# Cross attention in a two-layer decoder: scores from plain queries and keys of two heads at a time, in the two halves of the rows

## The reference, cut to what matters

```python
        q = lat @ Wq
        kv_input = jnp.concatenate([x, lat], axis=1)
        kv = kv_input @ Wkv
        k, v = jnp.split(kv, 2, axis=-1)
...
        dots = jnp.einsum('bhid,bhjd->bhij', q, k) * scale
        attn = jax.nn.softmax(dots, axis=-1)
        out = jnp.einsum('bhij,bhjd->bhid', attn, v)
```

## Time and profile before

| | us |
|---|---|
| median of 3 runs | 941.05 (939.36 to 941.20) |
| the profiled execution | 941.59, of it a span of 939.7 |
| busy in the span: PE / DVE / ACT / POOL | 847.7 / 561.1 / 480.4 / 256.1 |
| busy weight loads (PEld) | 695.7 |
| cross attention, from its first score to the first of its last unit | 132.2 to 519.1 |

### The profile page before, as it was taken

The page is one execution under the profiler, slowest core; times in us unless marked ns, Lnnn a source line. Parts: engine busy times, 40 slices in busy tenths (PEclk is TensorE's granted clock), DMA queues, the critical chain, the costliest instruction groups (busy, mean ns, idle before and its releaser), DMA issues.

```text
span 939.7 us, 19518 instructions
## 1 busy us (share of the span) xinstructions
PE 847.7 (90%) x6498; PEld 695.7 (74%) x6498; DVE 561.1 (60%) x1561; ACT 480.4 (51%) x1154; POOL 256.1 (27%) x541
## 2 busy tenths in 40 slices
PE   5999879999999999999999968885897888887788
PEld 3888668888888888888888756663796566665565
DVE  3876466555655566655655347774544577666474
ACT  2455465555555555555555315664464476677141
POOL 3864120000000000000000047551075577776110
PEclk9999999999999999999999989999899899999995
DMA  7000000000000000000000030001222000000000
GB/s 270 2 2 1 1 1 1 1 1 1 0 0 0 0 0 0 0 0 0 0 0 0 1 115 1 2 1 28 88 47 59 1 1 0 0 0 0 24 1 22
DMA packets 9410, 15.85 MB, mean 17 GB/s; under 512 B 816, under 2 KB 5040, under 8 KB 8976
## 3 DMA queue, kind: packets, MB, share of 16 engines
q1 hardware_dynamic: 8400, 13.23, 4.2%
q0 software_dynamic: 960, 1.97, 0.9%
HBM read 13.16 MB, written 2.03 MB: 16 GB/s over the span
## 4 chain that ended last, share of the span: by engine, by line
PE 76%; ACT 7%; DVE 6%; issue 6%; POOL 3%; DMA 1%; ACTq 1%; DVEq 0%; POOLq 0%; SPq 0%
PE psum L875 9%; PE psum L887 9%; PE psum L855 5%; PE psum L856 5%; PE psum L857 5%; PE psum L847 5%; PE psum L598 4%; ACT arena L1301 4%; PE psum L840 3%; PE psum L617 3%; PE psum L635 3%; PE psum L956 2%; PE psum L566 1%; PE psum L1034 1%; PE psum L648 1%
## 5 line engine op out<-in xcount | busy, mean ns | idle before, releaser
L1818 DVE TENSOR_REDUCE xnegmax<-psum 128x1 f32<-128x768 f32 x128 | 122.4, 956 | 139.5 <-PE psum L857 139.3
L1405 ACT ACTIVATE arena<-psum,xnegmax 128x768 f32<-128x768 f32 x128 | 115.5, 903 | 139.5 <-DVE xnegmax L1818 97.8
L2265 POOL COPY acur<-A_all 128x128 f32 (+1 forms) x18 | 5.2, 293 | 388.1 <-PE psum L840 388.1
L875 PE MATMUL psum<-pack_a,arena 128*128 128x128 f32 x768 | 106.8, 275 | 0.2 <-ACT arena L1396 0.2
L1249 ACT ACTIVATE arena<-psum 128x384 f32<-128x384 f32 (+1 forms) x128 | 69.5, 546 | 71.2 <-PE psum L620 42.1
L855 PE MATMUL psum<-kv_high,xq_high 128*128 128x384 f32 x256 | 101.5, 396 | 1.8 <-DVE kv_low L1813 1.6
L875 PEld LDWEIGHTS psum<-pack_a,arena 128*128 128x128 f32 x768 | 87.5, 141 | 13.9 <-issue 12.3
L1396 ACT ACTIVATE arena<-psum 128x512 f32<-128x512 f32 x128 | 75.9, 593 | 42.5 <-PE psum L875 42.5
L887 PE MATMUL psum<-arena,xv 128*64 128x256 f32 x768 | 89.9, 383 | 0.0
L856 PE MATMUL psum<-kv_low,xq_high 128*128 128x384 f32 x256 | 86.8, 339 | 0.0
L857 PE MATMUL psum<-kv_high,xq_low 128*128 128x384 f32 x256 | 86.7, 339 | 0.0
(11 more groups left out here) (309 smaller groups left out, 1853.6 us busy)
## 6 DMA issues: line engine op xcount, KB each, us to landing
w1all<-in_w SPq DMA_DIRECT2D x1, 2048.0 KB, 8.2
arena<-in_w SPq DMA_DIRECT2D x1, 2048.0 KB, 10.8
pack_v<-in_pack_v SPq DMA_DIRECT2D x1, 1088.0 KB, 9.0
pack_l<-in_pack_l SPq DMA_DIRECT2D x1, 1079.5 KB, 12.0
pack_q<-in_pack_q SPq DMA_DIRECT2D x1, 1024.0 KB, 6.9
pack_a<-in_pack_a SPq DMA_DIRECT2D x1, 653.0 KB, 6.1
pack_f<-in_pack_f SPq DMA_DIRECT2D x1, 556.0 KB, 9.9
x<-in_x SPq DMA_DIRECT2D x2, 256.0 KB, 3.0
```

The lines of the kernel that those rows point to most:

```text
L875: last = transpose(bank[4 + (3 * u + c) % 2][:, (2 * i + h) * P:(2 * i + h + 1) * P], xprob[:, u % 2, h * KEYS + kt * P:h * KEYS + (kt + 1 ...
L1405: activation(xprob[:, u % 2, half * KEYS:(half + 1) * KEYS].rearrange("p (c w) -> p c w", c=2), src, ACT.Exp, bias=xnegmax[:, u % 2, half: ...
L1818: v.tensor_reduce(xnegmax[:, u % 2, half:half + 1], banks_pair(half), AX.XY, ALU.max, negate=True)\
```

## The change

The head products `A_all` go away. For each pair of heads TensorE now forms plain queries (128 columns: two heads of 64) and plain keys of the 768 rows, the keys by three split matmuls for each half of 384 (`keys`), one such half in every unit, ahead of their use, in bank 7. Queries and keys are split again (`xq_high`, `k_high` by ScalarE, `xq_low`, `k_low` by VectorE), now inside the loop. A unit is now two heads with one tile of 128 queries: each head's product runs over 64 rows only, one in the lower and one in the upper half of the rows, into different PSUM banks, and all twelve score matmuls of a unit stand together. The key weights are split once ahead of the loop (`wk_all`), and GpSimd copies the two heads' columns for each pass.

```diff
-                def queries(it, u):
-                    pe.wait_ge(sx["acur_ready"], it * 2 + u % 2 + 1)
-                    mm(bank[6][:, T:2 * T], acur[:, u % 2, :], kvT[:, u // 2, S2:KEYS], start=True, stop=True)\
-                        .then_inc(sx["q_psum"], 1)
+                def queries(it, b):
+                    pe.wait_ge(sx["wq_ready"], it + 1)
+                    mm(bank[6][:, T:2 * T], wq_now[:, :], kvT[:, b, S2:KEYS], start=True, stop=True).then_inc(sx["q_psum"], 1)
+                def keys(it, b, c):
+                    pe.wait_ge(sx["wk_ready"], it + 1)
+                    out, some = bank[7][:, 0:W], slice(c * W, (c + 1) * W)
+                    mm(out, wk_now[:, 0, :], kv_high[:, b, some], start=True, stop=False)
+                    mm(out, wk_now[:, 0, :], kv_low[:, b, some], start=False, stop=False)
+                    mm(out, wk_now[:, 1, :], kv_high[:, b, some], start=False, stop=True).then_inc(sx["k_psum"], 1)
...
-                def scores(u, half):
+                def scores(u):
+                    tile, slot = slice(u % 2 * P, (u % 2 + 1) * P), u // 2 % 2
                     for c in range(2):
...
+                        some = slice(c * W, (c + 1) * W)
+                        for i, (q, k) in enumerate(((xq_high, k_high), (xq_high, k_low), (xq_low, k_high))):
+                            for a in range(2):
+                                head = slice(XD * a, XD * (a + 1))
+                                last = mm(bank[2 * a + c][:, 0:W], q[head, slot, tile], k[head, slot, some],
+                                          start=(i == 0), stop=(i == 2))
+                                if c == 1 and i == 2:
+                                    last.then_inc(sx["score_psum"], 1)
```

More of the change, by code:

```diff
@@ L116, in decoder @@
         x = sb("x", [P, NT, D])
+        with nc.sbuf_tensor("k_high", [P, 2, KEYS], f32r) as k_high, nc.sbuf_tensor("k_low", [P, 2, KEYS], f32r) as k_low:
+            pass
         z = sb("z", [P, NT, D])
@@ L927, in body @@
                                 if prev or u >= 4:
[L929 to L935, removed]
-                            if cur:
-                                pe.wait_ge(sx["q_ready"], n + 2)
-                            weighted(it * 4 + b - 1, (b - 1) % 4)
-                        if behind:
+                                    pe.wait_ge(sx["rb_ready"], p - 1)
+                                    pe.wait_ge(sx["y_done"], p)
+                                queries(*after)
+                            pe.wait_ge(sx["k_ready"], n + (4 if prev or u else 3))
+                            values(*after, odd)
+                            if not prev and u == 0:
+                                pe.wait_ge(sx["v_ready"], 3)
+                                keys(0, 1, 1)
+                        if behind and not odd:
+                            transposed(n - 1, (u - 1) % 8, (2,))
+                        if weigh and not odd:
+                            if cur:
+                                pe.wait_ge(sx["q_ready"], p + 2)
+                            weighted(p - 1, (b - 1) % 4, range(0, 2))
+                        if weigh and odd:
+                            weighted(p - 1, (b - 1) % 4, range(2, KT))
+                        if behind and odd:
                             transposed(n - 1, (u - 1) % 8, (2,))
-                        if weigh:
-                            factors(it * 4 + b - 1)
+                        if weigh and odd:
+                            factors(p - 1)
                         if not cur and u == 0:
@@ L1843, in body @@
                             dve.wait_ge(sx["pT_psum"], m * 3 + 2)
-                            v.tensor_copy(xpT[:, (mu // 2) % 2, mu % 2, 2 * T:4 * T], bank[4 + (3 * mu + 1) % 2][:, :])\
+                            v.tensor_copy(xpT_of(mu, 1), bank[4 + (3 * mu + 1) % 2].rearrange("p (k a q) -> p k a q", k=2, a=2))\
                                 .then_inc(sx["pT_dve"], 1)
+                        if cur:
+                            if not odd:
+                                query_low(it * 4 + b + 1, (b + 1) % 2)
+                            values(n + 3, (b + 1) % 4, odd)
+                            if not prev and u == 0:
+                                keys_low(4, 1, 1)
                         if not odd and ((prev and u == 0) or (cur and u)):
```

185 lines of the change are left out of this document (98 added, 87 removed).

## The result

The changed kernel takes 971.78 us (median of 4 runs, 969.67 to 972.88) against 941.12 (939.36 to 941.41): a ratio of 1.031, with a 95% interval of 1.0272 to 1.0348. It is slower, and by twice what was predicted: +30.7 by the medians instead of +15. The profiled execution took 970.9, with a span of 968.6, 28.9 more than before.

The account below looks back on a forecast made before the run. TensorE's work was taken as the bound, 12.315 us a pair. Profiled 941.6, plus 7.9 for two waits in 31 loop pairs, plus 6.9 for the start, gave 956 us; range 935 to 975.

Parts of the forecast that it names:

- the case that was held likeliest: Whole kernel: halves overlap and two waits per pair make it slower, 956 us, range 945 to 966, chance 0.53.
- TensorE's scores: Each unit, first score to first key: two row halves run at once, 1.26 us, bounds 1.06 and 2.31.
- The two waits: TensorE idles before values (0.13 even, 0.49 odd unit) for low keys, and 0.70 before the even weighted sum for low query.
- The rival of a shorter chain: Loop: scores to low query take less time than the rows say; pair 11.84, total 934 us, chance 0.20.
- The loop's sum: Loop: a pair takes 12.57 us, 0.255 more than before; over 31 pairs +7.9 us.
- The price of a switch: TensorE's row or column halves: 0.07 to 0.13 or 0.20 us each; seven a pair, 0.83 us in the sum.
- The start: Ahead of the loop and first unit: second unit starts at 144.2 instead of 137.32, +6.9 us, bounds +4.5 and +9.
- The rival of the clock: Loop: waits lower TensorE's granted clock for a tenth of it; 972 us, chance 0.12 together with further waits.
- No overlap: Score matmuls: the two halves don't run at once in fp32r, 2.31 us per unit; 1021 us, chance 0.07.
- nothing to see: Loop: chain shorter by just 0.24 us a unit, pair 12.1; total within 0.2% of before, chance 0.08.

Follow-up runs that it names:

- both heads in one half: The changed kernel with both heads' score matmuls in the lower half of the rows, the second head's scores left out: 1042.31 us in one run.
- the idle matmuls: The changed kernel plus nine matmuls with unread results in TensorE's waits ahead of the loop and in its first unit: 966.72 us.
- both moves: The changed kernel with the low query right behind the second maximum, high query before the first exponential, and odd units' weighted passes ahead of the values: 937.59 us.

## Why the prediction was right on the sign and wrong on the size

The measured 971.78 lies inside the range that was given, 935 to 975, but above the 945 to 966 of the case that was held likeliest. The mechanism came as forecast; two terms of the sum were too small.

- **TensorE's scores.** From first score to first key 1.24 (predicted 1.26). The halves overlap; shown with both heads in one half. That the sum of 1.26 came out is in part luck: it had six steps of 0.176 and a switch, and left out that the first step is 0.28, as the first of a group over all rows was 0.27 before.
- **The two waits.** They came at the places named, with the releasers named. The values of the odd unit start 1.95 behind the first key (predicted 1.98), the low query 3.29 (3.32). The rival of a shorter chain is out: the chain is as long as the rows made it.
- **The loop's sum was mis-sized: +7.9 predicted, +19.3 measured**, a pair of 12.94 instead of 12.57 (401.08 / 31). The pair above has 12.95, and its terms differ from the predicted ones by 0.38. *Low query to weighted sum:* 494.31 + 0.41 to 494.97 is 0.25, and I had taken a hand-over of 0.05; with the 0.04 that the low query is early, 0.16. TensorE's list has three waits in a row there, of which the low query is the first: the trace has two instructions of its queue, lines 890 and 892, at 494.8 and 494.9, and the weight load behind them at 494.94. Ahead of the values in the odd unit no such instruction stands between the low keys and the weight load, at 499.18. *Transposes and factors to the scores:* 0.80 (501.93 to 502.73) instead of 0.63, because from the factors to the first score it takes 0.31 (489.47 to 489.78) instead of 0.14 to matmuls over all rows before (501.76, below, to 501.90 in the earlier trace rows): 0.17. *Values and weighted sum of the odd unit:* 0.87 + 1.88 instead of 0.67 + 2.00, 0.08. *The even unit's weighted sum:* 1.02 instead of 1.05 - 0.07, 0.04; the rest, from the values' start and two times x, -0.07. No work was missing from the list; each term stands behind a wait or a switch, where I had prices from running work. The second unit, in part at the lower clock, has 1.1 of the 19.3 (6.28, against 5.19 with the idle matmuls).

```profile
501.76 0.38 PE L894 MATMUL psum<-pack_a,xrbc 128*128 128x128 f32 x2
```

- **The price of a switch** is the second of these. I took entering row halves at 0.07 from the head products; from the factors it is 0.17. The column halves of the weighted sum cost 0.18 behind their last pass (1.88 less 16 passes of 0.106), near the 0.20 that I had. Leaving the row halves costs less, about 0.09: the step from the last pair to the key is 0.27, where a step is 0.176. The Trainium skill's rule ("TensorEngine Tiling (Array Packing)", Key Properties) that changing the tiling mode drains TensorE, priced at a matmul's length beyond its step, 0.16, is near the first two of these and above the third; the trace agrees with it in part.
- **The start was mis-sized: +6.9 predicted, +9.5 measured.** A key half ahead of the loop takes what I worked out, 2.5 (132.73 to 135.20). The miss stands ahead of it and in the first unit: two groups of values at the lower level, so that the first score comes at 137.79 instead of 136.5, and another 1.3 in the first unit, where VectorE waits 0.52 for the high keys and 0.54 for the values that start at 142.51. I had read the low clock off the kernel before as a matter of its first scores; in the changed kernel it falls earlier and lasts longer. That the clock costs time there is shown: with idle matmuls the first unit takes 7.83 (136.95 to 144.78), where I had 7.7, instead of 8.99. That the missing head products are what lowers it was not tested.
- **The rival of the clock** was put in the wrong place: behind the second unit the granted clock of the loop stays at 1.00, and the lower level lies ahead of the loop and in its first two units. That its number, 972, is the one measured is chance. *No overlap* and *nothing to see* are out.
- **Where TensorE's saving went.** The pair without waits is 11.7 to 11.8, 0.5 to 0.6 less than before; both moves bring back most of it (11.86, 0.45 less). In the trace of both moves the loop's 31 pairs take 368.36 (147.55 to 515.91), 13.4 less than before, and the second unit starts 10.2 later; that is why it is worth under 1%.

What stays open: whether the weighted sum would start sooner behind the low query if the other two waits stood ahead of that one; the trace shows the order of the three, and no run changed it. Not tried: VectorE splits the other three batches just ahead of the first maximum, and these could be moved into its idle time ahead of the loop.

## What to carry to other kernels

When a unit's operands are made inside it, write down the chain from the first matmul to the last operand ahead of counting what the matmul engine saves: here 0.5 to 0.6 a pair was saved and 1.1 lost to two waits, and two moves in the lists gave it back. Price what stands behind a wait or a switch of halves with rows that stand behind one, not with steps of running work. And look at the granted clock when work is removed ahead of a loop: here matmuls that nobody needs, put into the waits that were left, gave 5 us.

## What the runs showed of the hardware

- Two row halves overlap though their matmuls stand three places apart in TensorE's list: 972.59 against 971.78 us, with the pairs starting together in the trace, so the fourth matmul in the list starts with the first. The Trainium skill ("TensorEngine Tiling (Array Packing)", Key Properties) says that tiles operate independently; the trace agrees, and the order of issue did not matter here.
- Nine matmuls whose results nobody reads made two kernels faster, by 5.1 and 5.6 us, since TensorE's granted clock then stayed at 1.00 through a stretch of many short waits where it had been 0.50 from 126 to 144 in the one and to 150 in the other.
